# Making the cross-attention keys between the experts of a decoder block, with Pool normalising them

## What is computed

```
x = layernorm(x + mamba_moe(x))          # selective scan, then 8 experts, top 2
x = layernorm(x + cross_attention(x, ctx))
x = layernorm(x + ffn_fp8(x))            # weights and rows rounded to fp8

# cross attention, 16 heads of 128, ctx of 4 x 64 tokens of width 128
k = rmsnorm((ctx @ Wk).reshape(B, Skv, H, D), gk);  v = ctx @ Wv
q = rmsnorm((x @ Wq).reshape(B, Sq, H, D), gq)
out = softmax(q @ k.T / sqrt(D)) @ v @ Wo

# FFN weights: rows reordered, scaled per row, rounded
w_scale = max(abs(W[:, idx]), axis=1) / 448;  qw = fp8(W[:, idx] / w_scale)
```

## Time and profile before

| what | value |
|---|---|
| median of 3 runs | 770.42 us (770.1 to 772.38) |
| profiled execution, its own time | 769.14 us |
| span of the profiled execution | 767.4 us |
| TensorE busy, weight load busy | 615.5 us (80%), 476.6 us (62%) |
| VectorE, ScalarE, Pool busy | 486.9, 382.2, 310.1 us |
| mean granted TensorE clock | 0.908 of full speed |

### The profile page before, as it was taken

How to read it: one execution, slowest core, us unless ns; L and a number is a source line. 1 busy time by engine, 2 the same in 40 slices (tenths; PEclk the granted TensorE clock), 3 DMA queues, 4 the chain that set the end, 5 groups by cost and what they waited for, 6 DMA issues and landing times.

```text
span 767.4 us, 11185 instructions
## 1 busy us (share of the span) xinstructions
PE 615.5 (80%) x3639; PEld 476.6 (62%) x3639; DVE 486.9 (63%) x738; ACT 382.2 (50%) x831; POOL 310.1 (40%) x251
## 2 busy tenths in 40 slices
PE   2998426777887789699989999997989999954652
PEld 1467126677777677598989989984845655542321
DVE  2686696999999975324443423336626577786995
ACT  4630977999999954421211111117635545523441
POOL 5402018999899995122323223230021232212221
PEclk9996858999999999899999999999999999985555
DMA  6000324111111106504432423116000000000001
GB/s 234 0 28 3 114 106 158 56 56 55 52 47 56 56 9 212 207 21 151 151 137 95 157 98 129 50 34 226 1 1 0 1 0 0 0 0 0 0 0 56
DMA packets 16936, 52.89 MB, mean 69 GB/s; under 512 B 2673, under 2 KB 8562, under 8 KB 15106
## 3 DMA queue, kind: packets, MB, share of 16 engines
q1 hardware_dynamic: 14066, 42.97, 15.5%
q0 software_dynamic: 2688, 7.34, 3.1%
q10 hardware_dynamic: 144, 2.10, 0.7%
HBM read 47.49 MB, written 4.92 MB: 68 GB/s over the span
## 4 chain that ended last, share of the span: by engine, by line
PE 51%; ACT 20%; DVE 12%; issue 10%; POOL 4%; DMA 2%; DVEq 1%; POOLq 0%; ACTq 0%
PE ps L1473 14%; ACT arena L537 9%; PE ps L1481 7%; PE ps L1549 7%; ACT arena L548 7%; PE ps L1241 4%; PE ps L1539 3%; PE ps L1568 3%; PE ps L1359 2%; PE ps L1519 2%; DVE x L1176 2%; POOL arena L366 1%; PE ps L1260 1%; POOL arena L376 1%; PE ps L1401 1%
## 5 line engine op out<-in xcount | busy, mean ns | idle before, releaser
L376 POOL TENSOR_TENSOR arena<-arena 128x1024 f32<-128x1024 f32 x64 | 151.1, 2373 | 9.3 <-DVE arena L860 7.6
L860 DVE TENSOR_TENSOR_SCAN arena<-arena,ps 128x1024 f32<-128x1024 f32 x64 | 146.0, 2285 | 14.0 <-POOL arena L376 7.5
L1473 PE MATMUL ps<-arena 128*128 128x128 f32 x1008 | 121.7, 282 | 6.7 <-DVE arena L980 5.3
L1473 PEld LDWEIGHTS ps<-arena 128*128 128x128 f32 x1008 | 119.4, 197 | 10.1 <-DVE arena L980 6.3
L613 ACT ACTIVATE arena<-ps 128x256 f32<-128x256 f32 x63 | 24.1, 383 | 148.9 <-PE ps L1473 148.9
L1317 PE MATMUL ps<-ident,arena 128*128 128x128 f32 x512 | 68.5, 277 | 29.9 <-ACT arena L548 21.7
L537 ACT ACTIVATE arena<-arena,a_neg 128x510 f32<-128x510 f32 x128 | 84.5, 707 | 11.4 <-DVE arena L860 7.8
L548 ACT ACTIVATE arena<-arena,b_tok 128x512 f32<-128x512 f32 x128 | 84.3, 707 | 1.7 <-DVE arena L851 1.7
L980 DVE TENSOR_TENSOR arena<-arena,ps 128x256 f32<-128x256 f32 x63 | 26.3, 421 | 90.9 <-ACT arena L613 87.0
L1317 PEld LDWEIGHTS ps<-ident,arena 128*128 128x128 f32 x512 | 54.9, 140 | 43.6 <-ACT arena L548 41.3
L1334 PE MATMUL ps<-ident,arena 128*128 128x128 f32 x544 | 71.9, 277 | 5.4 <-POOL arena L366 5.0
(11 more groups left out here) (273 smaller groups left out, 1063.7 us busy)
## 6 DMA issues: line engine op xcount, KB each, us to landing
arena<-in_w_moe SPq DMA_DIRECT2D x8, 2304.0 KB, 8.9
arena<-c_dram SPq DMA_DIRECT2D x32, 256.0 KB, 3.1
arena<-in_w_o ACTq DMA_DIRECT2D x1, 2048.0 KB, 8.8
arena<-in_w_qT SPq DMA_DIRECT2D x1, 2048.0 KB, 9.9
arena<-moe_out SPq DMA_DIRECT2D x4, 512.0 KB, 5.6
arena<-in_w_q SPq DMA_DIRECT2D x1, 2048.0 KB, 12.1
x<-in_x SPq DMA_DIRECT2D x1, 1024.0 KB, 5.8
arena<-in_w_in SPq DMA_DIRECT2D x1, 1024.0 KB, 7.8
```

The costliest lines, as they stand in the source:

```text
L376: pool.tensor_tensor(in_chunks(hC[:, unit % 2, :]), in_chunks(h[:, unit % 2, :]), c_bc[:, m % C_BUFS, :].unsqueeze(1).to_broadcast([P, 2, ...
L860: nc.vector.tensor_tensor_scan(h[:, k, :], dA[:, k, :], ps[:, 2 * k:2 * k + 2, :].rearrange("p a b -> p (a b)"), 0.0, ALU.mult, ALU.add).t ...
L1473: ins = nc.tensor.matmul(ps[:, bank, c * P:(c + 1) * P], w[:, k, at:at + P], xT[:, k, :], start=(k == 0), stop=(k == KD - 1))
```

## The change

Keys are made in quarters of four heads between the experts. At the head of experts 3 to 6 TensorE makes one quarter (2 products), ScalarE squares and copies it; one expert later VectorE sums the squares (`sum_squares`) and Pool takes the power -1/2 and multiplies (`normalise_keys`), ahead of that expert's turns. Quarters 0 and 1 are transposed at the head of experts 6 and 7, quarters 2 and 3 behind the experts, between the diagonals. Pool's single loop over all tiles becomes one loop for each expert. The 16 output steps lie 6, 4, 4 and 2 at experts 0 to 3 (two of the six behind the first transposed rows). FFN quantising has six parts in other places: weight 0's mask product among the routing tiles, weight 1's on Pool behind the first row gather. SP loads w_k and w_qT only when the first rows are transposed. The FP8 transposes use banks 2 and 3 and the transposes of w_down move to expert 4. TensorE waits at a border for the takes of its banks. Other places of the diff only move buffers.

```diff
-ARENA_KB = 181
+ARENA_KB = 187
...
-        VW_STEPS = [4, 2, 2, 0, 2, 0, 2, 0, 4]
-        FP8_TURNS = {3: 2, 5: 0, 7: 1}
+        VW_STEPS = {0: 6, 1: 4, 2: 4, 3: 2}
+        FP8_TURNS = {4: 2, 5: 0, 7: 1}
+        K_AT, KT_AT, QK_AT = 3 * PAIRS, 4 * PAIRS, 5 * PAIRS
+        QUARTERS = range(4)
+        K_TURNS, KT_TURNS, NORM_TURNS = {3 + q: q for q in QUARTERS}, {6: 0, 7: 1}, {4 + q: q for q in QUARTERS}
...
+            sp.wait_ge(s["xT_psum"], 2)
             load(w_k, inp["w_k"], "ld_k")
...
+            pool.wait_ge(s["gathered_w1"], FCH * 16)
+            pool.tensor_tensor(w_raw[1], w_raw[1], up_mask[:, :].unsqueeze(1).to_broadcast([P, FCH, D]), ALU.mult).then_inc(s["index_set"], 1)
             pool.wait_ge(s["xT_psum"], 2)
             gather_rows(row_of[:, 1:2])
...
-            total = pool.value_load(bounds[0:1, E:E + 1], min_val=E, max_val=OUT_TILES)
-            with pool.Fori(0, total) as j:
+
+            def normalise_keys(q):
+
+                pool.wait_ge(s["k_ms"], q + 1)
+                both_halves = lambda t: t[:, :].rearrange("p (j h) -> p j h", j=2)[:, :, 4 * q:4 * q + 4]
+                pool.tensor_tensor(both_halves(k_rs), both_halves(k_ms), neg_half[:, 0:8].rearrange("p (j h) -> p j h", j=2), ALU.pow).then_inc(s["k_normed"], 1)
+                pool.wait_ge(s["k_normed"], 2 * q + 1)
+                pool.wait_ge(s["kv_out"], K_AT + 2 * q + 2)
+                heads = k_raw.rearrange("p j (h d) -> p j h d", d=DH)[:, :, 4 * q:4 * q + 4, :]
+                pool.tensor_tensor(heads, heads, both_halves(k_rs).unsqueeze(3).to_broadcast([P, 2, 4, DH]), ALU.mult).then_inc(s["k_normed"], 1)
+
+            def move_rows(j):
...
+            last = 0
+            for e in range(E):
+                if e in NORM_TURNS:
+                    normalise_keys(NORM_TURNS[e])
+                first, last = last, pool.value_load(bounds[0:1, e + 1:e + 2], min_val=1, max_val=OUT_TILES)
+                with pool.Fori(first, last) as j:
+                    move_rows(j)
...
+            def take_keys(q, banks):
+
+                if q >= 2:
+                    act.wait_ge(s["k_ms"], q - 1)
+                for j in range(2):
+                    act.wait_ge(s["kv_psum"], K_AT + 2 * q + j + 1)
+                    nc.scalar.activation(k_sq[:, q % 2, j, :], ps[:, banks[j], :], ACT.Square, scale=float(DH) ** -0.5).then_inc(s["k_squared"], 1)
+                    nc.scalar.activation(k_raw[:, j, q * HALF:(q + 1) * HALF], ps[:, banks[j], :], ACT.Identity).then_inc(s["kv_out"], 1)
+
+            def take_transposed_keys(q, banks):
+                for half in range(2):
+                    n = 2 * q + half
+                    act.wait_ge(s["kv_psum"], KT_AT + n + 1)
+                    nc.scalar.activation(kT[:, 2 * n:2 * n + 2, :], ps[:, banks[half], :].rearrange("p (a b) -> p a b", a=2), ACT.Identity,
+                                         scale=gqk[:, 0:1]).then_inc(s["kv_out"], 1)
...
+                for n in range(VW_STEPS.get(e, 0)):
+                    take_values_times_output(step, (4, 5, 2, 3, 4, 5)[n] if e == 0 else 2 + n)
                     step += 1
+                if e in K_TURNS:
+                    take_keys(K_TURNS[e], (2, 3) if e in KT_TURNS else (4, 5))
+                if e in KT_TURNS:
+                    take_transposed_keys(KT_TURNS[e], (4, 5))
...
+            for m in range(3):
+                act.wait_ge(s["spread_psum"], 3 + m)
+                width = (FCH, FCH, KD)[m] * P
+                nc.scalar.activation(scale_rows[m], ps[:, 0:2, :].rearrange("p a b -> p (a b)")[:, 0:width], ACT.Identity).then_inc(s["spread_done"], 1)
+                if m < 2:
+                    take_transposed_keys(2 + m, (2 + 2 * m, 3 + 2 * m))
...
+                    quantise(0, (0,))
...
+            def sum_squares(q):
+
+                dve.wait_ge(s["k_squared"], 2 * q + 2)
+                for j in range(2):
+                    at = j * HEADS + 4 * q
+                    ins = nc.vector.tensor_reduce(k_ms[:, at:at + 4], k_sq[:, q % 2, j, :].rearrange("p (h d) -> p h d", d=DH), axis=AX.X, op=ALU.add)
+                link(ins)
+                both_halves = k_ms[:, :].rearrange("p (j h) -> p j h", j=2)[:, :, 4 * q:4 * q + 4]
+                nc.vector.tensor_scalar(both_halves, both_halves, 1e-5, None, ALU.add).then_inc(s["k_ms"], 1)
+
+            quantise(0, (1,))
...
+                if e in NORM_TURNS:
+                    sum_squares(NORM_TURNS[e])
+                if e < 2:
+                    quantise(0, ((2, 3), (4, 5))[e])
+                if e in (2, 3, 6):
+                    quantise(1, {2: (1, 2), 3: (3, 4), 6: (5,)}[e])
...
+            def keys(q, banks):
+
+                pe.wait_ge(s["ld_k"], 16)
+                for j in range(2):
+                    nc.tensor.matmul(ps[:, banks[j], :], ctxT[:, j * P:(j + 1) * P], w_k[:, q * HALF:(q + 1) * HALF], start=True, stop=True).then_inc(s["kv_psum"], 1)
+
+            def transpose_keys(q, banks):
+
+                pe.wait_ge(s["k_normed"], 2 * q + 2)
+                for half in range(2):
+                    for hd in range(2):
+                        for j in range(2):
+                            at = (4 * q + 2 * half + hd) * DH
+                            ins = nc.tensor.transpose(ps[:, banks[half], hd * KVT + j * P:hd * KVT + (j + 1) * P], k_raw[:, j, at:at + DH], ident[:, :])
+                    ins.then_inc(s["kv_psum"], 1)
+
+            for n in range(4):
                 pe.wait_ge(s["kv_out"], (3, 4, 7, 8)[n])
                 values_times_output(n, (4, 5, 2, 3)[n])
+            transpose_rows(0)
+            for n in range(4, VW_STEPS[0]):
+                pe.wait_ge(s["kv_out"], PAIRS + n - 3)
+                values_times_output(n, n)
             step = VW_STEPS[0]
-            transpose_rows(0)
-            pe.wait_ge(s["kv_out"], PAIRS + VW_STEPS[0])
+            pe.wait_ge(s["kv_out"], PAIRS + 4)
             pe.wait_ge(s["routed"], 1)
             for e in range(E):
+                taken = K_AT + 2 * K_TURNS[e] + 2 if e in KT_TURNS and e in K_TURNS else PAIRS + step + 2
                 if e in FP8_TURNS:
                     transpose_fp8(sorted(FP8_TURNS).index(e), FP8_TURNS[e])
-                for n in range(VW_STEPS[e] if e else 0):
-                    values_times_output(step, 4 + n)
+                for n in range(VW_STEPS[e] if 0 < e <= 3 else 0):
+                    values_times_output(step, 2 + n)
                     step += 1
+                if e in K_TURNS:
+                    keys(K_TURNS[e], (2, 3) if e in KT_TURNS else (4, 5))
+                if e in KT_TURNS:
+                    transpose_keys(KT_TURNS[e], (4, 5))
+                if e in (1, 2, 3, 6):
+                    pe.wait_ge(s["kv_out"], taken)
+                if e in FP8_TURNS:
+                    pe.wait_ge(s["wT_done"], 2 * sorted(FP8_TURNS).index(e) + 2)
...
+            for m in range(3):
+                pe.wait_ge(s["counted"], 3 + m)
+                if m:
+                    pe.wait_ge(s["spread_done"], 2 + m)
+                spread_diagonals(diag[m], (FCH, FCH, KD)[m], 0)
+                if m < 2:
+                    transpose_keys(2 + m, (2 + 2 * m, 3 + 2 * m))
+            kv[0] = QK_AT
```

More of the change, by code:

```diff
@@ L161, in build @@
         w_v, vT, w_o = view(119.5, [HEADS * DH]), view(131, [HEADS, KVT]), view(147, [HEADS, D])
-        w_k, k_raw, k_sq = view(40.5, [HEADS * DH]), view(131, [2, HEADS * DH]), view(147, [2, HEADS * DH])
+        w_k, k_raw, k_sq = view(40.5, [HEADS * DH]), view(131, [2, HEADS * DH]), view(48.5, [2, 2, HALF])
         kT = view(147, [HEADS, KVT])
@@ L181, in build @@
         w_size = [view(66.5, [FCH * D]), view(66.5, [FCH * D]), view(90, [KD * FF])]
-        w_fp8 = [view(34.5, [FCH, D], BF16), view(37.5, [FCH, D], BF16), view(116.5, [KD, FPAD], BF16)]
+        w_fp8 = [view(34.5, [FCH, D], BF16), view(37.5, [FCH, D], BF16), view(181, [KD, FPAD], BF16)]
         w_fp8T = [view(73.5, [KD, FPAD], BF16), view(76.5, [KD, FPAD], BF16), view(84.5, [FCH, D], BF16)]
@@ L602, in _ @@
             for e in range(E):
-                for n in range(VW_STEPS[e]):
-                    take_values_times_output(step, (4, 5, 2, 3)[n])
+                for n in range(VW_STEPS.get(e, 0)):
+                    take_values_times_output(step, (4, 5, 2, 3, 4, 5)[n] if e == 0 else 2 + n)
                     step += 1
+                if e in K_TURNS:
+                    take_keys(K_TURNS[e], (2, 3) if e in KT_TURNS else (4, 5))
+                if e in KT_TURNS:
+                    take_transposed_keys(KT_TURNS[e], (4, 5))
                 if e == 0:
@@ L775, in _, with quantise @@
             dve.wait_ge(s["spread_done"], 2)
-            def quantise(m, parts=(0, 1, 2)):
+            def quantise(m, parts=range(6)):
                 mask, chunks, width = ((up_mask[:, :], FCH, D), (up_mask[:, :], FCH, D), (down_mask[:, 0:FF], KD, FF))[m]
@@ L788, in quantise @@
```

(7 more changed lines are left out.)

81 lines of the change are left out of this document (11 added, 70 removed).

## The result

The changed kernel takes 766.55 us (median of 10 runs, 764.44 to 768.57) where the kernel before takes 770.36 on the same chip (10 runs, 767.87 to 772.38): ratio 0.9945, 95% interval 0.9934 to 0.9956, some 4 us. The profiled execution has a span of 764.8 us (before 767.4) at a mean granted clock of 0.910. The forecast was 764.3, a gain of 6.1 us. The sum was near, but its terms were not: three of the five missed by 3.8 to 5.9 us, in both directions.

What follows compares the result with a forecast made beforehand. TensorE's chain of waits was taken as the bound, with gaps before and behind the experts. 5.3 - 4.6 - 5.7 + 11.1 = 6.1 us gained, 764.3 us for the median; range 757 to 773, the forecast's own 760 to 768.

Steps and rivals of the forecast that it cites:

- the five: Forecast changes by stage: start -5.3 us, borders +4.6, stalls on Pool +5.7, tail -14.0, cold clock at the scores +2.9.
- Part 1: Start of the experts: loads behind the first rows let TensorE start near 318.9 at full clock; 5.3 us gained.
- Part 2: Seven borders between experts: added TensorE work makes them 23.4 us against 18.8; 4.6 us lost.
- Part 3: Pool's key normalising delays row gathers at experts 4, 5 and 6; stalls of 5.7 us, bounds 3.0 and 8.4.
- rival A: Pool's normalising is hidden, as rows land sooner or borders are longer; gives back 5.7 us: 758.6; chance 0.14.
- Part 4: From experts to attention: queries' product starts some 7.3 us after the experts, x comes last; 14.0 us gained, net 11.1.
- the cold clock: Attention's start: after TensorE's idle time, first scores and queries run 5.8 us at half clock; 2.9 us lost.
- x's chain last: Sign of being right, ahead of the attention: the chain that makes x ends last.
- B: Pool's normalising makes row gathers late at experts 4 to 6 and halves the clock: 14.3 us lost, 772.9; chance 0.19.
- C: Gain lost to a second gather 3.5 us late beside the loads and to cooling: 770.1, no change; chance 0.15.
- D: DMA queues take turns, so the second gather at the start isn't late: 1.0 us less, 763.3; chance 0.07.

Runs made afterwards that it cites:

- the version without stalls: Changed kernel with weight 1's mask product on VectorE, TensorE's waits in the loop, Pool's scatter wait behind the next row gather: 0.9753 of before (0.9817 with dummy products).
- product twice: Changed kernel with Pool's normalising product done twice, the first time into scratch: 1.0039 of the kernel before.
- loads alone: Kernel before with only the loads of w_k and w_qT moved behind the first transposed rows: 0.9947 of the kernel before.
- mask on VectorE: Changed kernel with weight 1's mask product moved from Pool back to VectorE: 0.9912 of the kernel before.
- loads back: Changed kernel with the loads of w_k and w_qT issued ahead of the first rows again: 0.9950 of the kernel before.
- short filler: Changed kernel with two dummy TensorE products ahead of the transposes of x and two behind: 0.9925 of the kernel before.
- keep warm: Changed kernel with dummy TensorE products around the transposes of x, three ahead, one behind each first pair, five behind all: 1.0033 of the kernel before.

## Why the prediction came out as it did

- **Part 1, start: mechanism right, one cost left out.** Rows alone land in 2.9 us (forecast 3.0); without Pool's mask product the experts start 5.4 us behind the gather (forecast 318.9 - 313.24 = 5.7), VectorE's first product comes 9.8 behind it (forecast 323.05 - 313.24 = 9.8), and the stage gains 5.5 (forecast 5.3). The step that failed is that of the mask on Pool: I charged its 3.6 us (measured 3.45) to the second gather alone, which it did not delay, and took VectorE's small products beside it at nothing. One of them waited for it, 4.0 us.
- **Part 2, borders: the work right, the waits wrong.** The forecast of 23.4 us for the work stands beside 21.0 in the version without stalls; mostly expert 6 was over-charged (4.0, measured 2.6), and two slips (3.7 + 0.3 is 4.0, not 4.05; 7.1 / 8 is 0.89, not 0.87) don't matter. "TensorE's on wT_done holds the expert's matmuls behind it, but VectorE's FP8 takes (1.1 to 1.8 us) end before the key products do" is the step that failed. The takes do end first (422.53 against 422.78); I asked whether the wait would be late, and not what the queue still has to do when it ends. Against the version without stalls, the borders with waits at the loop's head are 0.4 to 2.4 us longer each, 8.3 in all.
- **Part 3, Pool: rival A came true in the changed kernel, by the very cause that its text named,** longer borders, beside a shorter product (1.89 instead of 2.37 us) and an earlier landing (9.2 instead of 10.3). Take the long borders away and the stalls are there in the second tiles of experts 4, 5 and 6, the three that were named, with 4.0 to 4.1 us; with the fourth in the first tile of expert 5, which wasn't named, they cost 5.6 (26.59 - 21.00) where 5.7 was forecast. The price of Pool's work was right for the borders that the forecast assumed, and the changed kernel had others. So the miss in part 2 paid for the miss in part 3: 5.9 too little against 5.7 too much.
- **Part 4, tail: right.** 14.4 us gained for 14.0; the queries' product began 7.8 us behind the experts for 7.3; the cold clock cost 1.8 for 2.9, and only the first scores, not the queries (6.88 us, as before).
- **Rivals B to D.** B did not come, though the run with the product twice shows it one step further: 1.9 us more on Pool gave 1.0039. C's late second gather is real in the run with the loads alone, whose start lost 1.3 us of it (22.99 us from the first product to the end of expert 0, 21.72 with the mask on VectorE), but in the changed kernel the start was late already. D fell with the 8.0 us that the second gather took, in the changed kernel as in loads alone.

Of the signs that the prediction named for being right, two came (clock 1.00 at the first matmul, x's chain last) and three did not: the first matmul 5.7 us behind the gather (9.38), no ScalarE wait over 1 us at a border (2.10 at expert 6), and TensorE idle for rows at experts 4 to 6. That the total was near is luck: errors of 3.8 and 5.9 us one way and 5.7, 1.1 and 0.4 the other. Left open: why the clock falls in one execution and not in another behind the same idle time. Behind ScalarE's takes at expert 6, 2.1 us of idle time left it at 1.00 in the changed kernel, and in loads back and short filler the following 48 matmuls took 7.25 us instead of 5.62; behind the experts, 2.3 to 2.5 us of waiting for the last rows cooled the diagonals in some traces and not in others.

## What to carry to other kernels

A hidden cost has to be stated with the slack that hides it, because the mend of another term takes that slack away: here a gain of 8.3 us at the borders brought 5.6 us of late rows with it, until Pool's wait was moved too. A wait at the head of a loop cost TensorE here the loop's entry behind it even where it ended in time; put such a wait as late in the body as the data allow. Before a product is moved to Pool, list VectorE's instructions with two SBUF inputs beside it, and who waits for them. And when the clock decides a difference of 2 us, look at it in each trace before you give the difference to an edit.

## What the runs showed of the hardware

- One VectorE product of 128x64 took 4.28 us instead of 0.23 beside a Pool product of 3.45.
- Behind a wait that ends just ahead of it, entering a loop with bounds from memory left TensorE without work for 1.4 to 1.6 us, as issue that no semaphore explains, with 1.62 to 1.67 us from the end of the wait to the first matmul; with the wait inside the loop it is 0.01.
- Pool's in-place product of 128x1024 with a factor broadcast over 128 columns took 1.89 us; the one of L376, whose second operand is 512 columns read twice, took 2.37.
- A row gather of 128 rows takes 2.9 us alone and 7.4 to 8.0 beside two loads issued just before it or with it.
- The granted clock fell from 1.00 to 0.50 in all five traces with 1.6 to 2.0 us of idle time followed by the 16 transposes of x, and stayed at 1.00 in keep warm, where dummy products filled 1.6 us. Behind 0.69 us of idle time it stayed in four traces without dummies and fell in one.
